# Placing the heads of four engines' loops at the first slot of an instruction block, in a Mamba kernel with a mixture of experts

## The chip, the cores and the metric

The kernel runs on one core of one Trainium2 chip. The metric is the device time of one execution in microseconds. Before the change its median over three runs is 8184.05 us (8180.95 to 8189.45). All arithmetic that matters here is in f32.

## The reference, cut to what matters

The input x is 4 sequences of 1024 tokens with 256 features. It is normalised, and then goes two ways: through eight Mamba layers, one after another, and through a mixture of eight experts of which each token takes one. The result is x plus the product of the first with the silu of the second.

```python
def _mamba_layer(x, Wi, cw, cb, Wx, Wdt, bdt, Alog, Dp, Wo):
    xz = einsum('bld,ed->ble', x, Wi); xin, z = split(xz, 2)
    xin = silu(causal_conv(xin, cw, cb))
    x_dbl = einsum('blc,ec->ble', xin, Wx)          # dt_raw, Bm, Cm
    delta = softplus(einsum('blr,cr->blc', dt_raw, Wdt) + bdt)
    y = selective_scan(delta, Bm, Cm, xin, -exp(Alog), Dp)   # h = h*exp(d*A) + d*u*B ; y = h.C
    return einsum('blc,dc->bld', y * silu(z), Wo)
for i in range(8):
    x = x + _mamba_layer(x, ...)
```

The scan has 512 channels and 16 states, and it is run over 1024 tokens of each of the 4 sequences in each of the 8 layers.

## The kernel before

The program has three stages. `experts` (up to about 520 us of the span) normalises and runs the mixture; `mamba` (to about 8116 us) runs the layers; `finish` multiplies and adds. The change is in `mamba`.

In `mamba` the work is cut into 64 units, numbered from 0: 8 layers by 4 sequences by 2 halves of 512 tokens. An even unit is a first half (h = 0) and an odd one a second half, which takes the scan's carry of the first. One unit is 16 states by 4 channel blocks, which makes 64 tiles of 128 partitions by 512 tokens. For each tile GpSimd makes the drive (L850), ScalarE the decay exp(delta A) into PSUM (L891), VectorE the scan (L1037). TensorE turns the state (L1192, four transposes an item) into one of two PSUM places, ScalarE weighs it with C (L898), and TensorE turns it back and adds it up in ps_y (L1199, four more). Between these, at places written out by hand (RING_AT, CONV_AT and the like), stand the projections of the next units, the convolution, the softplus and the gate. VectorE ends what it does ahead of a new unit with the second of two du products (L1085), and has the alive scan (L1059) some 20 us into the unit; the text uses these two as marks.

Each engine runs its own instruction stream, and semaphores order them. On TensorE, VectorE, ScalarE and GpSimd the units come from `units`: unit 0 and unit 1 are written out, then a loop of 30 iterations has two units in its body (units 2 to 61), and units 62 and 63 are written out again. L707 is the loop's line: its hint (the first instruction of the body), its counter and the compare-and-branch that closes it have that line in the trace. The branch is taken 29 times, always between an odd unit and the even one behind it. SyncE's stream, with all data transfers, is written out without a loop.

```python
        def units(eng, unit):
            unit(0, 0, 0, "first")
            unit(1, 1, 0, "mid")
            with nc.Fori(1, ITERS - 1, 1, engines=[eng.engine], hint_back_edge=True) as it:
                for h in range(HALVES):
                    unit(HALVES * it + h, h, it, "mid")
```

The instructions of an engine are 64 bytes each and are fetched from memory in blocks while it runs. In the compiled program the loop body, from its hint to its branch, has 2609 instructions on TensorE, 752 on ScalarE, 599 on VectorE and 344 on GpSimd. Counted from the start of each engine's own stream (the labels, which aren't loaded, left out) the bodies begin at instruction 6301 on TensorE, 1317 on ScalarE, 1122 on VectorE and 549 on GpSimd, and TensorE's branch is its instruction 8909. What the loader puts ahead of a stream comes on top of these and isn't in the program.

Of the kernel before, what the change touches and what calls it, by code (L numbers as in the profile page):

```python
# [40 lines left out]
ITERS = LAYERS * BATCH  # L41
# [596 lines left out]
def mamba(nc, w_in, w_x, w_dt, w_out, par, xres, ident, alive_dram, bc_dram):  # L638

    with ExitStack() as ctx:  # L640
# [62 lines left out]
        def units(eng, unit):  # L703

            unit(0, 0, 0, "first")
            unit(1, 1, 0, "mid")
            with nc.Fori(1, ITERS - 1, 1, engines=[eng.engine], hint_back_edge=True) as it:  # L707
                for h in range(HALVES):
                    unit(HALVES * it + h, h, it, "mid")
            unit(UNITS - 2, 0, ITERS - 1, "near")  # L710
            unit(UNITS - 1, 1, ITERS - 1, "last")
# [77 lines left out]
        def _(pool):  # L789
# [87 lines left out]
            halo(0, 0)  # L877
            mask_x(0, "pre1", 1, 1, 0)
            units(pool, unit)

        @block.scalar
        def _(act):
# [130 lines left out]
            exponent(0, 0, 0)  # L1013
            exponent(0, 0, 1)
            units(act, unit)
            for t in range(TC):
                weigh(UNITS, 0, "end", ("S", "prev", t), UNITS - 1, STATES - 1, t)

        @block.vector
        def _(dve):  # L1020
# [147 lines left out]
            for n in range(STATES):  # L1168
                for j in range(CB):
                    early(0, 1, "pre1", 1, 0, n, j)  # L1170
            units(dve, unit)
            for j in range(CB):
                gate(UNITS - 1, 1, j)
# [298 lines left out]
```

## Time and profile before

| | |
|---|---|
| median of 3 runs | 8184.05 us (8180.95 to 8189.45) |
| the profiled execution | 8167.01 us, span 8165.3 us |
| TensorE matmul, weight load | 6880.2 us (84%), 4850.8 us (59%) |
| VectorE | 6901.2 us (85%) |
| ScalarE | 6464.0 us (79%) |
| GpSimd | 6099.8 us (75%) |
| granted TensorE clock, mean | 0.959 |
| data transfers | 42 GB/s, 13.4% of the 16 engines' span |

The shares say how busy an engine is, not which one sets the time: no engine is full, and in each stretch of a unit another one comes last. The clock is a share of full speed, so that 0.5 is 1.2 GHz and 1.0 is 2.4 GHz. "issue" as a releaser means that the engine waited for nothing that the profile shows. Rows with a q behind the engine's name are of its sequencer.

### The profile page before, as it was taken

How to read it: one execution, taken by the hardware profiler on the slowest of the kernel's cores; microseconds unless marked ns; L12 is line 12 of the kernel's file. 1: busy time of each engine (PE TensorE's matmuls, PEld its weight loads, DVE VectorE, ACT ScalarE, POOL GpSimd, SP SyncE). 2: the span in 40 equal slices, each digit the busy share in tenths (PEclk: the TensorE clock that was granted, in tenths of full speed). 3: DMA queues.
4: the chain of work that ended last, by engine and by line, in shares of the span. 5: the costliest groups of instructions: out<-in, count | busy, mean ns of one | idle time of the engine just before them, and what ended most of it. 6: DMA issues, size and time to landing. Idle time of an engine off the chain costs nothing. (4 is left out here: it accounts for less than half of the span.)

```text
span 8165.3 us, 143446 instructions
## 1 busy us (share of the span) xinstructions
PE 6880.2 (84%) x39487; PEld 4850.8 (59%) x39551; DVE 6901.2 (85%) x6768; ACT 6464.0 (79%) x10250; POOL 6099.8 (75%) x5301
## 2 busy tenths in 40 slices
PE   6968888888888888888888888888888888888887
PEld 4645665565566556556655655665566566556555
DVE  3258988888898898889888888988888898888888
ACT  2258888888888888888888888888888888888887
POOL 2147787778788777778877777887778778778775
PEclk9979999999999999999999999999999999999998
DMA  4111111111111111111111111111111111111112
GB/s 155 33 34 37 37 37 42 39 36 38 39 42 40 35 38 42 39 36 38 38 41 39 36 38 39 41 40 36 36 42 40 36 38 39 40 39 37 37 37 88
DMA packets 201759, 345.60 MB, mean 42 GB/s; under 512 B 25152, under 2 KB 59744, under 8 KB 200832
## 3 DMA queue, kind: packets, MB, share of 16 engines
q1 hardware_dynamic: 197168, 325.46, 13.4%
q0 software_dynamic: 3792, 10.38, 0.4%
q8 instruction: 392, 6.42, 0.3%
q14 instruction: 407, 3.33, 0.1%
HBM read 318.04 MB, written 17.72 MB: 41 GB/s over the span
## 5 line engine op out<-in xcount | busy, mean ns | idle before, releaser
L850 POOL TENSOR_TENSOR drive<-du,brep 128x512 f32<-128x512 f32 x4096 | 5611.6, 1396 | 857.6 <-DVE du L1085 641.0
L891 ACT ACTIVATE ps_d<-delta,cur 128x512 f32<-128x512 f32 x4096 | 2827.5, 690 | 879.7 <-DVE state L1037 859.9
L898 ACT ACTIVATE prod<-ps_r,bcT 128x512 f32<-128x512 f32 x4096 | 2786.9, 680 | 353.6 <-PE ps_r L1192 343.0
L1192 PE MATMUL ps_r<-ident,state 128*128 128x128 f32 x16384 | 2613.4, 284 | 535.8 <-ACT prod L898 305.1
L1037 DVE TENSOR_TENSOR_SCAN state<-ps_d,carry,drive 128x512 f32<-128x512 f32 x2048 | 2519.5, 1265 | 281.7 <-ACT ps_d L891 143.5
L1037 DVE TENSOR_TENSOR_SCAN state<-ps_d,drive 128x512 f32<-128x512 f32 x2048 | 2398.4, 1205 | 395.1 <-ACT ps_d L891 203.3
L1199 PE MATMUL ps_y<-ident,prod 128*128 128x128 f32 x16384 | 2546.0, 281 | 106.5 <-issue 87.1
L1199 PEld LDWEIGHTS ps_y<-ident,prod 128*128 128x128 f32 x16384 | 1990.7, 145 | 773.2 <-issue 592.9
L1192 PEld LDWEIGHTS ps_r<-ident,state 128*128 128x128 f32 x16384 | 1906.0, 145 | 843.2 <-ACT prod L898 510.3
L1232 PE MATMUL ps_r<-xm,w_inx_sb 128*128 128x512 f32 x1024 | 529.9, 643 | 185.9 <-ACT prod L898 178.2
L1076 DVE SCALAR_TENSOR_TENSOR xc<-xpad,taps,xc 128x512 f32<-128x512 f32 x768 | 662.3, 862 | 2.9
L1240 PE MATMUL ps_r<-xm,w_inz_sb 128*128 128x512 f32 x1024 | 510.2, 621 | 126.1 <-ACT prod L898 125.8
L1269 PE MATMUL ps_r<-relu,w_out_sb 128*128 128x512 f32 x1024 | 468.4, 600 | 5.7 <-ACT prod L898 3.0
L1232 PEld LDWEIGHTS ps_r<-xm,w_inx_sb 128*128 128x128 f32 x1024 | 178.8, 194 | 377.3 <-issue 195.3
L836 POOL COPY carry<-state 128x4 f32<-128x4 f32 x512 | 175.1, 342 | 299.2 <-DVE state L1037 296.7
L1262 PE MATMUL ps_r<-xdbl,w_dt_sb 16*128 16x512 f32 x512 | 307.1, 682 | 80.6 <-ACT soft L944 51.4
L1240 PEld LDWEIGHTS ps_r<-xm,w_inz_sb 128*128 128x128 f32 x1024 | 174.6, 190 | 313.1 <-ACT prod L898 169.2
L1210 PE MATMUL ps_y<-u,skip 128*128 128x512 f32 x512 | 291.1, 711 | 20.7 <-DVE relu L1135 20.6
L1269 PEld LDWEIGHTS ps_r<-relu,w_out_sb 128*128 128x128 f32 x1024 | 184.2, 190 | 200.1 <-issue 187.0
L1248 PE MATMUL ps_r<-u,w_x_sb 128*48 128x512 f32 x512 | 236.4, 606 | 54.5 <-ACT u L916 54.5
L532 ACT ACTIVATE hid<-ps_t,b_sb 128x128 f32<-128x128 f32 x312 | 84.8, 382 | 227.5 <-PE ps_t L493 227.5
L460 POOL DMA_INDIRECT ys_dram<-yb,row x39 | 37.4, 958 | 296.7 <-DVE yb L552 296.7
(148 smaller groups left out, 4481.4 us busy)
## 6 DMA issues: line engine op xcount, KB each, us to landing
brep<-bc_dram SPq DMA_DIRECT2D x1024, 256.0 KB, 3.2
w_sb<-w SPq DMA_DIRECT2D x8, 1024.0 KB, 18.7
w_all<-w SPq DMA_DIRECT2D x8, 1024.0 KB, 13.7
xb<-xs_dram SPq DMA_DIRECT2D x39, 128.5 KB, 2.0
w_all<-x SPq DMA_DIRECT2D x4, 1024.0 KB, 9.3
w_inx_sb<-w_in SPq DMA_DIRECT2D x8, 512.0 KB, 4.0
w_inz_sb<-w_in SPq DMA_DIRECT2D x8, 512.0 KB, 4.0
w_out_sb<-w_out SPq DMA_DIRECT2D x8, 512.0 KB, 3.9
```

Source lines behind the costliest of these rows:

```text
L850: nc.gpsimd.tensor_tensor(drive[:, k % DRIVE, :], du[:, j, :], brep[:, n % BREP, :], ALU.mult).then_inc(drive_set, 1)
L891: nc.scalar.activation(ps_d[:, k % 2, :], delta[h][:, j, :], ACT.Exp, scale=cur[h][:, a:a + 1]).then_inc(decay_set, 1)
L898: nc.scalar.activation(prod[:, t, :], ps_r[:, item_place(U, h, kind, item), :], ACT.Copy, scale=bcT[(h + 1) % 2 if item[1] == "prev" else ...
L1037: nc.vector.tensor_tensor_scan(state[n % 2][:, j, :], ps_d[:, k % 2, :], drive[:, k % DRIVE, :], carry[:, n, j:j + 1] if h == 1 else 0.0, ...
L1076: step = nc.vector.scalar_tensor_tensor(xc[:, j, :], xpad[:, j, tap:tap + T], w, xc[:, j, :], ALU.mult, ALU.add)
L1192: last = nc.tensor.transpose(out[:, j * P:(j + 1) * P], state[n % 2][:, j, t * P:(t + 1) * P], ident[:])
L1199: last = nc.tensor.matmul(ps_y[:, j, t * P:(t + 1) * P], prod[:, t, j * P:(j + 1) * P], ident[:], start=False, stop=True, is_transpose=Tru ...
L1210: last = nc.tensor.matmul(ps_y[:, j, :], skip[:, j, :], u[:, j, :], start=True, stop=True, skip_group_check=True)
L1232: last = nc.tensor.matmul(out, w_inx_sb[:, k, j * P:(j + 1) * P], xm[h][:, k, :], start=(k == 0), stop=(k == DB - 1))
L1240: last = nc.tensor.matmul(out, w_inz_sb[:, k, j * P:(j + 1) * P], xm[hf][:, k, :], start=(k == 0), stop=(k == DB - 1))
L1262: nc.tensor.matmul(out, w_dt_sb[:, j * P:(j + 1) * P], xdbl[0:RANK, :], start=True, stop=True).then_inc(ring_ready, 1)
L1269: last = nc.tensor.matmul(out, w_out_sb[:, j, k * P:(k + 1) * P], gated[:, j, :], start=(j == 0), stop=(j == CB - 1))
```

## The change

The loop gets one more argument, which asks the loader to put the body's first instruction, on each of the four engines, at slot 0 of a block of 256 instruction slots (and so of a block of 128 as well). The slots skipped ahead of it are padding, and the stream jumps over them once. No instruction in the body is added, removed or moved against another, and no wait or buffer changes.

```diff
-            with nc.Fori(1, ITERS - 1, 1, engines=[eng.engine], hint_back_edge=True) as it:
+            with nc.Fori(1, ITERS - 1, 1, engines=[eng.engine], hint_back_edge=True,
+                         head_slot={eng.engine: 0}) as it:
                 for h in range(HALVES):
                     unit(HALVES * it + h, h, it, "mid")
```

## Rows read from the trace of the kernel before

**Rows 1.** The page, DMA queues of kind instruction: packets, MB, share of 16 engines.
```profile
q8 instruction: 392, 6.42, 0.3%
q14 instruction: 407, 3.33, 0.1%
```
**Rows 2.** Line L707 by engine: count, ns min/median/max, first and last start in us.
```profile
L707 PEldq COMPARE_BRANCH  x30: 87/3588/3933, 998.0 to 7899.1; - x30
...
L707 ACTq COMPARE_BRANCH  x30: 44/49/68, 998.6 to 7899.8; - x30
...
L707 DVEq COMPARE_BRANCH  x30: 61/68/90, 995.6 to 7896.7; - x30
...
L707 POOLq COMPARE_BRANCH  x30: 44/49/70, 983.5 to 7884.7; - x30
```
**Rows 3.** The waits: who waited for what, us in total, times, longest.
```profile
PE ps_y L1199 <- issue: 87.1, 26, 3.7
```
**Rows 4.** Timeline of PE around the turn into unit 14: start, length, instructions, idle before.
```profile
2181.25 0.62 PE L1192 MATMUL ps_r<-ident,state 128*128 128x128 f32 x4
...
2187.39 0.66 PE L1192 MATMUL ps_r<-ident,state 128*128 128x128 f32 x4 [1.12 <-ACT zs L910]
2191.59 1.11 PE L1199 MATMUL ps_y<-ident,prod 128*128 128x128 f32 x4 [3.54 <-issue]
```
**Rows 5.** The DMA view of 2187.4 to 2188.6 us, the instruction queue.
```profile
q8 instruction: 1, 0.02, 7.6%
```
**Rows 6.** Line L707 on TensorE's sequencer, 2184 to 2192 us.
```profile
L707 PEldq COMPARE_BRANCH  x1: 3823/3823/3823, 2187.5 to 2187.5; - x1
```
**Rows 7.** The DMA view of 2899 to 2900 us, ahead of the turn into unit 20.
```profile
q8 instruction: 1, 0.02, 7.5%
```
**Rows 8.** Line L707 on TensorE's sequencer, 2898 to 2903 us.
```profile
L707 PEldq COMPARE_BRANCH  x1: 1397/1397/1397, 2900.8 to 2900.8; - x1
```
**Rows 9.** Timeline of PE behind the turn into unit 20.
```profile
2905.66 0.33 PE L1192 MATMUL ps_r<-ident,state 128*128 128x128 f32 x1 [1.30 <-issue]
```
**Rows 10.** Windows: stretch, length, busy PE PEld DVE ACT POOL, clock, DMA share, GB/s.
```profile
2191.00:2194.00 3.00, 2.41 (x12) 2.41 (x13) 1.41 (x2) 0.31 (x1) 3.00 (x4) 0.50 0.30 79
...
2902.00:2905.00 3.00, 1.85 (x15) 1.62 (x15) 3.00 (x4) 1.88 (x4) 3.00 (x3) 1.00 0.03 8
```
**Rows 11.** Timeline of DVE: du and alive marks, turns into units 2, 14, 15, 20, 23.
```profile
757.82 1.20 DVE L1085 TENSOR_TENSOR du<-delta,u 128x1024 f32<-128x1024 f32 x1
778.57 1.19 DVE L1059 TENSOR_TENSOR_SCAN alive<-ps_r,zeros 128x512 f32<-128x512 f32 x1
...
2187.20 1.19 DVE L1085 TENSOR_TENSOR du<-delta,u 128x1024 f32<-128x1024 f32 x1
2211.98 1.19 DVE L1059 TENSOR_TENSOR_SCAN alive<-ps_r,zeros 128x512 f32<-128x512 f32 x1
...
2308.40 1.20 DVE L1085 TENSOR_TENSOR du<-delta,u 128x1024 f32<-128x1024 f32 x1
2330.36 1.25 DVE L1059 TENSOR_TENSOR_SCAN alive<-ps_r,alive,zeros 128x512 f32<-128x512 f32 x1
...
2900.54 1.19 DVE L1085 TENSOR_TENSOR du<-delta,u 128x1024 f32<-128x1024 f32 x1
2923.70 1.19 DVE L1059 TENSOR_TENSOR_SCAN alive<-ps_r,zeros 128x512 f32<-128x512 f32 x1
...
3257.51 1.20 DVE L1085 TENSOR_TENSOR du<-delta,u 128x1024 f32<-128x1024 f32 x1
3284.58 1.28 DVE L1059 TENSOR_TENSOR_SCAN alive<-ps_r,alive,zeros 128x512 f32<-128x512 f32 x1 [0.97 <-PE ps_r L1223]
```
**Rows 12.** Timeline of DVE: more du marks, into units 3, 12 and 13.
```profile
875.06 1.20 DVE L1085 TENSOR_TENSOR du<-delta,u 128x1024 f32<-128x1024 f32 x1
...
1950.73 1.19 DVE L1085 TENSOR_TENSOR du<-delta,u 128x1024 f32<-128x1024 f32 x1
...
2070.79 1.20 DVE L1085 TENSOR_TENSOR du<-delta,u 128x1024 f32<-128x1024 f32 x1
```

## The prediction

> **What bounds the kernel now.** I read the page first. It has no full engine, so the shares don't decide, and its chain of waits covers only the last 50 us. The change touches nothing but where code lies, so I then looked for rows of instruction fetch and of the loop's own line. The page has two queues of kind instruction. One moves 6.42 MB in 392 packets, which is 16.4 KB each, or 256 instructions of 64 bytes; the other 3.33 MB in 407, or 128 instructions each [rows 1]. I take the first queue to be TensorE's, since only TensorE executes enough instructions to fill it (16384 of one kind alone), and the second to be the other engines'.
>
> The view of line L707 shows what closing the loop costs. On ScalarE, VectorE and GpSimd the branch takes 49, 68 and 49 ns. On TensorE its median is 3588 ns and its longest 3933; only the last, which isn't taken, is 87 ns [rows 2]. The waits show the same from the other side: 26 idle times of TensorE with no releaser, 87.1 us in all [rows 3]. Of the 29 taken branches 26 are like the one at 2187.5 us and 3 are like the one at 2900.8.
>
> In the long case TensorE has 3.54 us with nothing to do [rows 4], while the branch stands for 3.82 us [rows 6] and one 16 KB packet of its queue is moved [rows 5]. The packet starts behind the branch's start. In the short case the packet starts between 2899 and 2900 us [rows 7], ahead of the branch at 2900.8, and the branch takes 1.40 us [rows 8]. A fetch that only a missed branch can start can't begin ahead of the branch. So I read it this way: the hint works, the block of the target is fetched once the sequencer is in the branch's own block, but TensorE enters that block only a few instructions ahead of the branch. The counts allow it. TensorE's branch is instruction 8909, and 35 blocks are 8960, so if the loader puts about 51 to 60 instructions ahead of the stream the branch lies in one of the first slots of its block. This offset is inferred, not shown.
>
> **What a turn costs.** The stall reaches the time if VectorE is late by it. I take the two marks on VectorE on either side of the turn [rows 11]:
> - long branch (unit 14): 2187.20 to 2211.98, 24.78 us; 25 of the 26 long ones lie within 0.05 us of it, one has 25.12.
> - short branch (unit 20): 2900.54 to 2923.70, 23.16 us; the other two are within 0.02.
> - no branch (unit 2, the same code, entered from straight code): 757.82 to 778.57, 20.75 us.
>
> So a long turn costs 24.78 - 20.75 = 4.03 us, more than the branch itself, and a short one 23.16 - 20.75 = 2.41 us. Two further rows say why it is more. Behind a long branch TensorE's clock is at 0.50, that is at 1.2 GHz, after the idle stretch; behind a short one it is at 1.00, 2.4 GHz [rows 10]. And behind the short one TensorE stops again for 1.30 us with no releaser [rows 9], some 36 instructions into the body, where by the same offset it crosses into the next block, whose fetch could only start once the head's block was there.
>
> **The change part by part.** *TensorE.* With the head at slot 0 the body of 2609 ends 2608 slots on; 10 blocks are 2560, so the branch is at slot 48 of its block. Counting 48 instructions back from the branch through weight loads and matmuls leads into the group at 2181.25 us [rows 4], 6.2 us ahead of the branch at 2187.5 [rows 6]. The fetch needs what the long branch takes, 3.9 us at most with the packet. It is hidden with 2.3 us to spare; without that cover up to 3.9 us a turn would remain. The branch should take about 0.09 us, its untaken price [rows 2]. The first crossing behind the head moves from some 40 to 256 instructions on, so the stop of 1.30 us goes too. What is late next at the turn is what is late in unit 2. Sum: 26 x 4.03 + 3 x 2.41 = 112.0 us gained. The bound from below is the mark distance of a turn between halves with no branch, unit 15, 2308.40 to 2330.36 = 21.96 us [rows 11]: 26 x 2.82 + 3 x 1.20 = 76.9 us. I take unit 2, since unit 15 has scans with a carry and other code.
>
> *The rest of an even unit.* From mark to mark unit 2 takes 875.06 - 757.82 = 117.24 us [rows 11, 12], so 96.49 behind its alive scan. Unit 14 takes 2308.40 - 2187.20 = 121.20, so 96.42. Unit 12 takes 2070.79 - 1950.73 = 120.06, and with the same first part 95.28 [rows 11, 12]. Which of the two an even unit gets depends on where low-clock stretches fall, and the change moves them. Of the 26 even units behind long branches the mean of this part is 95.6. If all became like unit 2, 29 x 0.9 = 26 us of the gain would be lost; if all became like unit 12, 29 x 0.3 = 9 us would come on top. I take no change and keep both ends: 86 to 121 us.
>
> *ScalarE, VectorE, GpSimd.* They lose nothing now [rows 2], so nothing can be gained at their branches. With heads at slot 0 their branches lie 111, 86 and 87 slots into blocks of 128 (752, 599 and 344 less one, less whole blocks). An iteration of some 238 us over 752 slots gives ScalarE 0.3 us a slot, so its last block is entered some 35 us ahead. The work of those slots hides a fetch of 3.9 us; if it didn't, it would be up to 3.9 us a turn. I set it at 0.
>
> *Entering the loop.* One jump over padding on each engine, once. If its target block isn't there it is one fetch, 0 to 3.9 us. I take 2 us, as ScalarE feeds every scan.
>
> *Data transfers.* SyncE has no loop and isn't touched; its waits come sooner with the rest.
>
> Net: 112 - 2 = 110 us. The profiled execution would go from 8167.0 to 8057 us. The median of the runs is 17 us above it, an offset that I keep: 8184.05 - 110 = 8074 us.
>
> **A page's rule against the change.** The same rows 2 show three engines whose loops are longer than what one or two blocks hold (ScalarE's 752 are 5.9 blocks of 128) and which still branch back in 49 to 68 ns. The Trainium skill, Runtime: NRT & Kernel Launch, section Instruction fetch mechanics, says that a taken branch to a target outside the current two-page window forces a fetch before execution can go on. By that rule TensorE's branch would stall wherever the head lies, and the time would stay at 8184 us; the trace disagrees with it on three engines out of four.
>
> **The rivals.**
> - *The turn still waits* (the head isn't moved, or TensorE's fetch starts at the branch in any layout). For it: 26 packets start behind the branch. Against it: the 3 that start ahead of it, and three engines that don't wait. Time 8184 us. Chance 0.07.
> - *The turn becomes like the one between halves*: another engine takes over at 21.96 us. Net 76.9 - 2 = 75, time 8109 us. For it: no branch stands between halves either, and those turns are at 21.96 us. Against it: unit 2, the same code as all even units, at 20.75. Chance 0.08.
> - *Slower: low-clock stretches early in the units.* Unit 23 has no branch and still takes 3284.58 - 3257.51 = 27.07 us between marks, with a wait for TensorE at its end, 5.1 us more than unit 15 [rows 11]. If shorter iterations lock to a phase in which one unit of every iteration has this, it costs 30 x 5.1 = 153 us against 110 gained: 8227 us. It decides from 22 of 30 iterations on. Only units 3 and 23 of 64 have it now. Chance 0.03.
> - *The forecast*, 8074 us, with its own range of 8063 to 8100 by the ends above. Chance 0.82.
>
> **How the numbers follow.** The range takes the forecast's ends, some us for the offset between profile and runs, and the second rival: 8055 to 8115 us. It leaves out the first and third, 0.10. A measurement of this kernel can tell about 0.2%, 16 us, from no change. Faster by more: 0.82 + 0.08 = 0.90. Within: 0.07. Slower: 0.03.
>
> **What would show it.** TensorE's branches near 0.09 us; the row of 26 idle times without a releaser gone; even units at about 20.75 us between the marks; the clock at 1.00 behind the turn. Branches still above 1 us would refute the reading of the offset; branches at 0.09 us with the marks at 22 us or more would mean that another engine took over; a gain at the turns that is lost again behind the alive scan would be the clock. I am wrong outright if another engine's branch grows to microseconds.

## The result, and the profile after

| | before | after |
|---|---|---|
| median | 8180.95 us (5 runs, 8177.64 to 8189.45) | 8153.57 us (5 runs, 8142.65 to 8172.95) |
| the profiled execution | 8167.01 us, span 8165.3 | 8159.41 us, span 8157.4 |
| mean clock | 0.959 | 0.959 |

The ratio is 0.9966, with an interval of 0.995 to 0.9983. The kernel is faster by 27 us, not by the 110 that I predicted, and the time lies above the range of 8055 to 8115. Behind L707 the lines are one higher than before: the scan is now L1038, the alive scan L1060, du L1086, the transposes L1193 and L1200.

The page's queues of kind instruction and the loop's line, as in [rows 1, 2]:

```profile
q8 instruction: 363, 5.95, 0.3%
q14 instruction: 381, 3.12, 0.1%
...
L707 POOLq COMPARE_BRANCH  x31: 33/49/70, 740.0 to 7878.1; - x31
L707 DVEq COMPARE_BRANCH  x31: 57/68/92, 752.3 to 7890.1; - x31
L707 PEldq COMPARE_BRANCH  x31: 88/3359/3895, 754.8 to 7892.5; - x31
L707 ACTq COMPARE_BRANCH  x31: 38/49/73, 755.5 to 7893.1; - x31
```

The head did move. Each engine has one branch record more, the jump over the padding, and TensorE fetches 29 packets fewer, 11 instead of 12 per trip, because a body of 2609 instructions that starts at slot 0 touches 11 blocks. But TensorE's branch still has a median of 3359 ns. The row of the waits that was to vanish is nearly what it was in [rows 3]:

```profile
PE ps_y L1200 <- issue: 86.1, 28, 3.7
```

The turn into unit 14, the counterpart of [rows 4 to 6]: timeline of PE, TensorE's branch, the instruction queue in the DMA view of 2182.8 to 2184 us, and the two marks on DVE.

```profile
2181.84 0.66 PE L1193 MATMUL ps_r<-ident,state 128*128 128x128 f32 x4 [1.12 <-ACT zs L911]
2185.57 1.11 PE L1200 MATMUL ps_y<-ident,prod 128*128 128x128 f32 x4 [3.07 <-issue]
...
L707 PEldq COMPARE_BRANCH  x1: 3351/3351/3351, 2181.9 to 2181.9; - x1
...
q8 instruction: 1, 0.02, 5.2%
...
2181.65 1.19 DVE L1086 TENSOR_TENSOR du<-delta,u 128x1024 f32<-128x1024 f32 x1
2206.44 1.19 DVE L1060 TENSOR_TENSOR_SCAN alive<-ps_r,zeros 128x512 f32<-128x512 f32 x1
```

The DMA view of 2175 to 2182.8 has no packet of q8. So the packet of the target starts behind the branch's start, as before. The turn is 24.79 us long, as before (24.78).

The turn into unit 18 is one of three with a short branch, the counterpart of [rows 7 to 9]. Its packet is in the DMA view of 2656.5 to 2658.2 us, ahead of the branch.

```profile
q8 instruction: 1, 0.02, 4.0%
...
L707 PEldq COMPARE_BRANCH  x1: 1140/1140/1140, 2658.3 to 2658.3; - x1
...
2658.20 0.66 PE L1193 MATMUL ps_r<-ident,state 128*128 128x128 f32 x4 [1.12 <-ACT zs L911]
2659.71 0.65 PE L1200 MATMUL ps_y<-ident,prod 128*128 128x128 f32 x4 [0.86 <-issue]
2660.20 0.60 PE L1193 MATMUL ps_r<-ident,state 128*128 128x128 f32 x4
...
2658.00 1.19 DVE L1086 TENSOR_TENSOR du<-delta,u 128x1024 f32<-128x1024 f32 x1
2678.78 1.19 DVE L1060 TENSOR_TENSOR_SCAN alive<-ps_r,zeros 128x512 f32<-128x512 f32 x1
```

This turn is 20.78 us, where the short ones before were 23.16 [rows 11]. The second stop of 1.30 us [rows 9] is gone: the first crossing into a new block now lies 256 instructions into the body. The windows behind the two turns (columns as in [rows 10]) show the clock at 1.2 GHz behind the long branch and at 2.4 GHz behind the short one:

```profile
2186.00:2189.00 3.00, 3.00 (x16) 3.00 (x15) 0.89 (x2) 1.27 (x2) 3.00 (x3) 0.50 0.42 92
2660.00:2663.00 3.00, 2.73 (x26) 2.50 (x25) 3.00 (x3) 1.98 (x4) 3.00 (x3) 1.00 0.03 5
```

Where the time of the two profiled executions went, from the marks of the 29 even units behind a branch: the turns' mean fell from 24.62 to 24.35 us (7.8 us in all), the rest of the even units rose from 95.57 to 95.97 (11.6 lost), the odd units fell by 0.17 each (4.8), and all that lies outside gives some 6. That makes 7 of the 7.6 us between the two executions. The medians are 27 us apart. The profiled execution of before, 8167.0 us, is shorter than each of its five runs (8177.6 to 8189.5), which that of after isn't; how many of the branches are short in executions without a profile isn't known, and so the other 20 us have no rows.

### The profile page after: what moved, and what is told of

Read it like the earlier page. It is cut to its first block and busy times, and to the rows that moved or that the text cites. A ratio compares the mean times of both kernels' runs of the same rounds, so it can differ in the third digit from the quotient of the medians.

```text
span 8157.4 us, 143514 instructions
## 1 busy us (share of the span) xinstructions
PE 6897.5 (85%) x39551; PEld 4858.0 (60%) x39551; DVE 6894.2 (85%) x6768; ACT 6470.4 (79%) x10250; POOL 6107.9 (75%) x5301
## 5 line engine op out<-in xcount | busy, mean ns | idle before, releaser
L1193 PE MATMUL ps_r<-ident,state 128*128 128x128 f32 x16384 | 2611.0, 284 | 523.2 <-ACT prod L899 302.4
L1038 DVE TENSOR_TENSOR_SCAN state<-ps_d,carry,drive 128x512 f32<-128x512 f32 x2048 | 2521.3, 1266 | 279.0 <-ACT ps_d L892 144.7
L1038 DVE TENSOR_TENSOR_SCAN state<-ps_d,drive 128x512 f32<-128x512 f32 x2048 | 2399.9, 1206 | 397.2 <-ACT ps_d L892 215.6
L1200 PE MATMUL ps_y<-ident,prod 128*128 128x128 f32 x16384 | 2554.2, 282 | 105.2 <-issue 86.1
L1200 PEld LDWEIGHTS ps_y<-ident,prod 128*128 128x128 f32 x16384 | 1995.8, 145 | 779.6 <-issue 597.6
L1193 PEld LDWEIGHTS ps_r<-ident,state 128*128 128x128 f32 x16384 | 1909.6, 145 | 828.1 <-ACT prod L899 507.5
```

Source lines behind the costliest of these rows:

```text
L1038: nc.vector.tensor_tensor_scan(state[n % 2][:, j, :], ps_d[:, k % 2, :], drive[:, k % DRIVE, :], carry[:, n, j:j + 1] if h == 1 else 0.0, ...
L1193: last = nc.tensor.transpose(out[:, j * P:(j + 1) * P], state[n % 2][:, j, t * P:(t + 1) * P], ident[:])
L1200: last = nc.tensor.matmul(ps_y[:, j, t * P:(t + 1) * P], prod[:, t, j * P:(j + 1) * P], ident[:], start=False, stop=True, is_transpose=Tru ...
```

## The experiments

All edits are made to the kernel after. E1 to E4 share their runs of before (median 8163.15 us), E5 to E8 theirs (8164.28), E9 to E11 theirs (8157.26); E12 has its own (8160.68). The four groups ran on four chips, and the change's own before is 8180.95, so that ratios are compared across them and not microseconds. Branches, packets and turns are read from one profiled execution of each kernel. A crossing is the place where TensorE's stream passes from one block of 256 slots into the next, and a block is entered when the first instruction behind the crossing is executed. The question is why a fetch whose block was entered 6.2 us ahead of the branch still comes late, and from where on it doesn't.

**E1: TensorE's head at slot 128, its branch at slot 176.**

```diff
-                         head_slot={eng.engine: 0}) as it:
+                         head_slot={eng.engine: 128 if eng.engine == mybir.EngineType.PE else 0}) as it:
```

> TensorE's loop head is at slot 128 of its block of 256 instead of slot 0, so that its closing branch (2608 instructions on) is at slot 176 instead of 48. The other three heads stay at slot 0. Theory A (the fetch for the hinted target starts only some 40 to 110 instructions after the branch's block is entered, as the fetches behind the other block crossings of the changed kernel do): all 29 branches near 0.09 us, turns into even units at 20.8 us between the marks, 26 x 4.0 us less than the changed kernel, so about 8153.6 - 104 = 8050 us. Theory B (on TensorE the fetch of a hinted target waits for the branch itself, and the three early ones are chance): 26 branches still at 3.3 to 3.9 us, time 8154 us.

Measured: 8035.87 us (8034.94 to 8040.89), ratio 0.9845 (0.9829 to 0.9861). Line L707, the instruction queue in the DMA view of 2143.5 to 2145 us, the branch of the same turn, and its marks:

```profile
L707 PEldq COMPARE_BRANCH  x31: 88/357/382, 758.6 to 7765.9; - x31
...
q8 instruction: 1, 0.02, 3.9%
...
L707 PEldq COMPARE_BRANCH  x1: 357/357/357, 2159.4 to 2159.4; - x1
...
2159.11 1.20 DVE L1086 TENSOR_TENSOR du<-delta,u 128x1024 f32<-128x1024 f32 x1
2179.85 1.19 DVE L1060 TENSOR_TENSOR_SCAN alive<-ps_r,zeros 128x512 f32<-128x512 f32 x1
```

The packet of the target starts 15 us ahead of the branch in all 29 turns, the row of idle time without a releaser is gone, and every turn is as long as the one of unit 2 before, 20.74 to 20.86 us. The Trainium skill, Runtime: NRT & Kernel Launch, section Instruction fetch mechanics, would make a taken branch with its target outside a two-page window wait for a fetch. Here 29 branches go back over ten blocks in at most 0.38 us, so the measurement decides against that rule for a loop with a hint.

**E2: TensorE's head at slot 64, branch at slot 112.**

```diff
+                         head_slot={eng.engine: 64 if eng.engine == mybir.EngineType.PE else 0}) as it:
```

> TensorE's loop head at slot 64, the closing branch at slot 112. Theory A: the fetch starts ahead of the branch in most or all turns, but may not have ended; branches between 0.09 and some 1.5 us, turns at 20.8 us, time 8050 to 8080 us. Theory B: 8154 us, branches at 3.3 to 3.9 us.

Measured: 8050.09 us (8044.98 to 8064.71), ratio 0.9859 (0.9842 to 0.9875).

```profile
L707 PEldq COMPARE_BRANCH  x31: 88/367/1708, 756.9 to 7792.0; - x31
```

The 29 branches fall into two groups. In 15 the packet starts 12 us ahead, and they take 0.36 to 0.38 us; in 14 it starts 1.3 us ahead, and they take 1.04 to 1.71 us. The block of the branch was entered 10 us ahead in both. So the lag from the entry to the start of the fetch differs from turn to turn: -2 us in 15 of them, 8.6 to 9.1 in 14. The profiled execution took 8064.71 us and is the longest of the four, so the median of 8050 may stand for turns that divide otherwise.

The short stops also show what a stop costs. Turns into units 16 and 20: windows behind the branch, the branches, and the marks of unit 20.

```profile
2399.00:2402.00 3.00, 3.00 (x21) 3.00 (x19) 3.00 (x4) 2.54 (x5) 3.00 (x4) 0.66 0.16 29
2868.70:2871.70 3.00, 2.56 (x22) 2.08 (x21) 3.00 (x3) 2.99 (x5) 3.00 (x3) 1.00 0.16 48
...
L707 PEldq COMPARE_BRANCH  x1: 1039/1039/1039, 2396.4 to 2396.4; - x1
L707 PEldq COMPARE_BRANCH  x1: 1064/1064/1064, 2866.0 to 2866.0; - x1
...
2865.68 1.19 DVE L1086 TENSOR_TENSOR du<-delta,u 128x1024 f32<-128x1024 f32 x1
2886.46 1.19 DVE L1060 TENSOR_TENSOR_SCAN alive<-ps_r,zeros 128x512 f32<-128x512 f32 x1
```

Two stops of the same length, 1.04 and 1.06 us. With the clock at 2.4 GHz behind it the turn is 20.78 us, as without a stop; where a stretch at 1.2 GHz follows, it is 23.18. All 14 divide so: nine at full clock have 20.76 to 20.79 us, five with the low clock 23.17 to 24.82. A stop of up to 1.55 us at full clock is covered.

**E3: head at slot 192, branch at slot 240.** The edit is that of E1 with 192.

> TensorE's loop head at slot 192, the closing branch at slot 240; the first crossing behind the head comes after 64 instructions. Theory A: branches near 0.09 us as with slot 128; the first crossing is short of room, so a stop of TensorE of up to 1.3 us some 60 instructions behind the turn may come back, without the half clock: turns at 20.8 to 21.5 us, time 8050 to 8070 us. Theory B: 8154 us.

Measured: 8037.78 us (8034.97 to 8041.59), ratio 0.9845 (0.9828 to 0.9861); branches `88/357/382`, turns 20.78 us. The packet starts 14.0 to 20.7 us ahead of the branch in all 29 turns. The first crossing, now 64 instructions into the body, costs nothing either: the stop that was expected as possible didn't come, and the time is below the expected 8050 to 8070.

**E4: only TensorE's head is placed, at slot 0.**

```diff
+                         head_slot={eng.engine: 0} if eng.engine == mybir.EngineType.PE else None) as it:
```

> Only TensorE's head is at slot 0; ScalarE's, VectorE's and GpSimd's lie where they fall, as in the kernel before. Both theories: the three other branches cost 0.05 to 0.07 us before and after, so their heads are worth nothing, and the time is that of the changed kernel, 8154 us, within 10 us. If the gain of 27 us came from the other engines' heads, it is 8181 us.

Measured: 8139.57 us (6 runs, 8131.59 to 8147.29), ratio 0.9971 (0.9958 to 0.9983), the same as the change's 0.9966 within the intervals; 25 long branches and 4 short. In microseconds it is 14 below the expected 8154, on a chip where before is 18 lower too. The other three heads bring nothing that can be measured.

**E5 and E6: the two sides of the block's edge.** Heads at slots 207 and 208 put the branch at slot 255 and at slot 0 of the next block. The edit is that of E1 with 207 and with 208.

> TensorE's head at slot 207, its branch at slot 255, the last of its block: the block is entered 255 instructions ahead of the branch. Theory A (lateness of the block's entry decides): branches at 0.36 us as with slots 128 and 192, turns at 20.8 us, ratio to the kernel before 0.985. Rival C (it is the first crossing behind the head, 49 instructions on, that decides, or the place near the block's end): as the kernel before, ratio 1.0, branches at 3.3 us or more.

> TensorE's head at slot 208, one slot further, its branch at slot 0 of the next block: the block is entered with the branch itself. Theory A: the fetch can't have started, 26 or more of 29 branches at 3.3 us or more, turns at 24.8 us, ratio to the kernel before 1.00, some 125 us slower than slot 207. Rival C: like slot 207.

Measured: E5 8039.06 us (8036.4 to 8046.41), ratio 0.9846 (0.9829 to 0.9862). E6 8162.21 us (10 runs, 8143.43 to 8163.55), ratio 0.999 (0.9981 to 1.0). L707 of E5 above, of E6 below, with E6's waits and its instruction queue:

```profile
L707 PEldq COMPARE_BRANCH  x31: 88/357/382, 758.5 to 7777.4; - x31
```

```profile
L707 PEldq COMPARE_BRANCH  x31: 87/3555/3834, 758.5 to 7898.1; - x31
...
PE ps_y L1200 <- issue: 95.3, 29, 3.6
...
q8 instruction: 393, 6.44, 0.3%
```

One slot is worth 123 us. Blocks of 256 slots are real, they are counted as the change counts them, and a branch at the first slot of a block is late 29 times of 29. This fits the kernel before, whose branch was in one of the first slots of its block by the stop of [rows 9].

**E7: slot 128, and no hints on any engine.**

```diff
-            with nc.Fori(1, ITERS - 1, 1, engines=[eng.engine], hint_back_edge=True,
-                         head_slot={eng.engine: 0}) as it:
+            with nc.Fori(1, ITERS - 1, 1, engines=[eng.engine], hint_back_edge=False,
+                         head_slot={eng.engine: 128 if eng.engine == mybir.EngineType.PE else 0}) as it:
```

> Heads as in the run with slot 128, but without the hints at the loop's top (one instruction less in each body). Theory A: a hint with a late fetch is worth no more than no hint. TensorE's 29 branches at 3.3 to 3.9 us, turns at 24.8 us or more, and ScalarE's and VectorE's branches at 3 us or more too, GpSimd's at 0.05 us (its body is not refetched). Ratio 1.00 to the kernel before where the stalls overlap, up to 1.01 where VectorE's own comes on top. If the hint is without effect on TensorE: 0.985.

Measured: 8162.24 us (10 runs, 8156.16 to 8178.7), ratio 1.0 (0.999 to 1.0009). L707 and the two queues:

```profile
L707 PEldq COMPARE_BRANCH  x31: 83/3697/4070, 759.2 to 7905.9; - x31
L707 ACTq COMPARE_BRANCH  x31: 38/45/54, 759.9 to 7906.6; - x31
...
q8 instruction: 393, 6.44, 0.3%
q14 instruction: 437, 3.58, 0.1%
```

Without the hint all of E1's gain is gone, and TensorE moves one packet more per trip than E1 (393 against 365): this fits a fetch that runs on into the block behind the loop and goes to the target only once the branch is executed. The hint turns it in time. ScalarE's branch record stays at 45 ns although its target isn't there: its next record of L707 comes 2.7 us behind the branch in the median, VectorE's 2.9, against 0.41 and 0.52 with the hint. In this view a short branch doesn't prove that nothing waited, and my reading of [rows 2] for the three other engines rested on it. The edit takes the hint from all four engines, so the time alone doesn't say which of them costs; TensorE's records and turns of 24.8 us, as before, do.

**E8: TensorE's head at 128, VectorE's at slot 46**, which puts VectorE's branch at slot 4 of a block of 128.

```diff
+                         head_slot={eng.engine: {mybir.EngineType.PE: 128, mybir.EngineType.DVE: 46}.get(eng.engine, 0)}) as it:
```

> TensorE's head at slot 128 as in the fastest run so far, and VectorE's at slot 46, so that VectorE's branch lies at slot 4 of a block of 128 (46 + 598 = 5 x 128 + 4). Theory A, if it holds for VectorE: its 29 branches go from 0.07 to some 3 us, and the time rises by 29 x 2 to 29 x 3.5 us, to about 8036 + 60 to 100 = 8096 to 8136 us. If its fetch isn't late or another wait hides it: 8036 us.

Measured: 8033.03 us (8031.62 to 8054.5), ratio 0.9847 (0.983 to 0.9865). L707 on VectorE in one turn of E8, and in the same turn of E1:

```profile
L707 DVEq COMPARE_BRANCH  x1: 68/68/68, 2159.4 to 2159.4; - x1
L707 DVEq BRANCH_PREFETCH_HINT  x1: 39/39/39, 2161.7 to 2161.7; - x1
```

```profile
L707 DVEq COMPARE_BRANCH  x1: 68/68/68, 2157.1 to 2157.1; - x1
L707 DVEq BRANCH_PREFETCH_HINT  x1: 39/39/39, 2157.6 to 2157.6; - x1
```

From branch to hint it is 2.30 us in the median (2.23 to 2.48), against 0.52. VectorE's sequencer is late by some 1.8 us a turn, and the mean turn stays at 20.77 us. VectorE has a scan and a product queued when it branches, about 2.4 us, behind the one that runs. The delay also bears on the block's size: in blocks of 256 this branch would be at slot 132, about 50 us behind the crossing at 238 us for 599 slots (an estimate), and no delay would be expected.

**E9 and E12: slots between.** Heads at 32 and 96, branches at slots 80 and 144. The edit is that of E1 with 32 and with 96.

> Head of TensorE's loop at slot 32 of a block of 256 (branch at slot 80), the other heads at 0. The loop branch has been seen at slots 48, 112 and 176: 3, 15 and 29 of 29 target packets started ahead of it. Theory 'the place of the branch in its block sets how much time the fetch has, and its start lags the entry of the block by a time that varies from turn to turn': slot 80 lies between 48 and 112, so 4 to 14 of 29 branches under 2 us, turn mean between 24.35 and 21.53, time between 8050 and 8150, most likely near 8110. Theory 'every branch that is not a whole further block away misses alike, and the 15 of slot 112 are chance': 3 or 4 early, 8150.

> Head of TensorE's loop at slot 96 of a block of 256 (branch at slot 144), the other heads at 0. So far the branch at slots 48, 80, 112 and 176 gave 3, 12, 29 and 29 of 29 branches under 2 us, and 0, 4, 15 and 29 of 29 under 0.5 us; the fetch started up to some 10 us behind the entry of the block. Theory 'the branch must lie far enough behind the crossing to cover that lag, and more distance always helps': at slot 144 at least 25 of 29 under 0.5 us, no branch above 1.7 us, turns of 20.78 to 21.2, 8034 to 8046 us, ratio 0.985. Rival 'what counts is where in the body the crossing falls, not the distance': any number of branches under 0.5 us, also fewer than 15, and a time anywhere from 8036 to 8100.

Measured: E9 8104.64 us (8100.71 to 8132.94), ratio 0.9945 (0.9927 to 0.9963). E12 8040.74 us (8037.9 to 8055.41), ratio 0.9858 (0.9842 to 0.9875). L707 of E9, then of E12:

```profile
L707 PEldq COMPARE_BRANCH  x31: 88/3099/3612, 757.3 to 7835.9; - x31
```

```profile
L707 PEldq COMPARE_BRANCH  x31: 88/438/461, 756.3 to 7773.1; - x31
```

These fill the curve. "Entered" is how long ahead of the branch TensorE executed the first instruction of the branch's block (good to some 0.4 us, since matmuls and the sequencer's records lie a few places apart); the fetch's start is that of the target's packet against the branch's start; both come from the records of TensorE's instructions and of its instruction queue, 29 turns each.

| run | slot | entered | fetch starts (turns) | under 0.5 / to 2 / over 2 us | mean turn | median |
|---|---|---|---|---|---|---|
| E6 | 0 | 0 | +0.9 to +1.4 (29) | 0 / 0 / 29 | 24.76 | 8162 |
| after | 48 | -6.1 | +0.7 to +1.5 (26), -1.3 (3) | 0 / 3 / 26 | 24.35 | 8154 |
| E9 | 80 | -8.0 | +0.7 to +1.3 (17), -1.3 (8), -5.6 to -7.0 (4) | 4 / 8 / 17 | 23.04 | 8105 |
| E2 | 112 | -10.0 | -0.9 to -1.4 (14), -12 (15) | 15 / 14 / 0 | 21.53 | 8050 |
| E12 | 144 | -13.7 | -5.7 to -7.0 (28), -12.6 (1) | 29 / 0 / 0 | 20.96 | 8041 |
| E1 | 176 | -15.2 | -15.3 to -15.8 (29) | 29 / 0 / 0 | 20.78 | 8036 |
| E3 | 240 | -20.0 | -14.0 to -20.7 (29) | 29 / 0 / 0 | 20.78 | 8038 |
| E5 | 255 | -21.7 | -15.7 to -23.8 (29) | 29 / 0 / 0 | 20.79 | 8039 |

Slot 80 gave 12 branches under 2 us, inside the 4 to 14 of the first theory, and slot 144 gave 29 of 29. The more slots lie between the crossing and the branch, the fewer turns are late, and from 144 on none is. The rival of E12, that only the place in the body counts, isn't needed for the branches, but it isn't dead for the lag: that is -2 to 9 us from E2's crossing, 4.8 to 7.6 from the change's, and about zero from E1's.

**E10: only TensorE's head is placed, at slot 128.**

```diff
+                         head_slot={eng.engine: 128} if eng.engine == mybir.EngineType.PE else None) as it:
```

> Only TensorE's head is placed, at slot 128 (branch at slot 176); ScalarE, VectorE and GpSimd stay where the kernel before has them. Theory 'only TensorE's branch is waited for': as with all four placed, 8036 (8033 to 8042), ratio 0.985, branches of 0.36 us, turns of 20.78. Rival 'with TensorE's stop gone the other engines' branches are next in line, and their heads at slot 0 helped': 8045 to 8060.

Measured: 8043.21 us (8035.24 to 8046.52), ratio 0.986 (0.9844 to 0.9877). That is one us above the upper end of the expected 8033 to 8042, with an interval that overlaps E1's; the profiled execution has a span of 8033.5 us against E1's 8034.1, branches `88/357/382` and turns of 20.77. One head on one engine is the whole effect.

**E11: TensorE's head at 128, ScalarE's at slot 21**, which puts ScalarE's branch at slot 4 of a block of 128.

```diff
+                         head_slot={eng.engine: {mybir.EngineType.PE: 128, mybir.EngineType.Activation: 21}.get(eng.engine, 0)}) as it:
```

> TensorE's head at 128; ScalarE's head moved so that its branch stands at slot 4 of a block of 128, only four instructions behind the crossing. Both theories expect ScalarE's next own record to come late behind its branch, some 2.3 us instead of 0.41, as it did on VectorE with its branch at slot 4. Theory 'work already queued on the engine covers it': VectorE had 2.4 us queued and lost nothing; ScalarE has one or two activations of about 0.7 us queued, so 1 to 1.7 us per turn come to light and 29 turns cost 0 to 45 us, most likely 30: 8066. Rival 'ScalarE has slack in the turn whatever is queued': 8036 as with the head at 0.

Measured: 8043.04 us (8037.96 to 8050.77), ratio 0.9857 (0.984 to 0.9873), against E10's 8043.21 on the same chip: no cost in the medians. The profiled execution, 8050.77 us, has two turns of 25.8 us, with the clock at 1.2 GHz late in the turn and branches of 0.36 us. L707 on ScalarE in one turn of E11, and in the same turn of E1:

```profile
L707 ACTq COMPARE_BRANCH  x1: 49/49/49, 2161.9 to 2161.9; - x1
L707 ACTq BRANCH_PREFETCH_HINT  x1: 31/31/31, 2162.7 to 2162.7; - x1
```

```profile
L707 ACTq COMPARE_BRANCH  x1: 49/49/49, 2160.1 to 2160.1; - x1
L707 ACTq BRANCH_PREFETCH_HINT  x1: 31/31/31, 2160.5 to 2160.5; - x1
```

Both theories had expected a delay of some 2.3 us, and it is 0.3 to 0.6. So the run doesn't tell them apart: the cover was hardly asked for. It shows only that four slots behind a crossing were nearly enough on ScalarE, which takes about 0.3 us per slot, where on TensorE 48 slots weren't.

## Why the prediction was wrong

**Right: the branch is the cost, and the hint can remove it.** E1 takes the branches to 0.36 us and E7 puts them back.

**Right: the price of a turn and its bound.** I took 4.03 us for a long turn, from unit 2's 20.75. In E1 the mean turn is 20.78 against 24.62 before, 29 x 3.84 = 111.4 us, where my sum had 112.0. E1's medians are even 127 us apart, and the spans of the two profiled executions 131. These say where the rest is: the odd units are shorter by 0.52 us each in the mean (15 us) and the first units by 5. The rival in which another engine takes over at 21.96 us fell with this.

**Right: the stop behind the short branch.** With the head at slot 0 it is gone, and the three short turns are at 20.78 us.

**Right: the other engines' heads.** E4 and E10 show them worth nothing. The reason that I gave, "they lose nothing now", leaned on the branch's own record, which E7 shows to be blind on ScalarE and VectorE. It holds all the same: in the kernel before, the next own record comes 0.41 and 0.52 us behind the branch, against 2.7 and 2.9 where the fetch is late.

**Wrong: "The fetch needs what the long branch takes, 3.9 us at most with the packet. It is hidden with 2.3 us to spare."** This one step carries nearly the whole error. The fetch itself is shorter than I said: from the packet's start to the end of the branch it is 2.3 to 2.8 us in the kernels before and after. But I let it start with the entry of the block. In the kernel after the block is entered 6.1 us ahead and the packet starts 6.8 to 7.6 us behind that in 26 of 29 turns, some 1 us behind the branch's start. I had no row for the time between entry and start, and took it as nothing without saying so. The trace of before did have it. With the block's edge where the stop of [rows 9] puts it, some 36 to 40 instructions into the body, each trip has eleven crossings, and by the records the packets start between 3.8 us ahead of the crossing instruction and 8.8 behind it; at one crossing the median is 8.2 us. Set against the 6.2 us of cover, these would have said that slot 48 is too early.

**The sum redone.** Three short turns at 20.78 instead of three at 23.15, and 26 long ones as before: 7 us, which is what the turns of the profiled executions give (7.8).

**The rival that came closest** was "the turn still waits", at 0.07, but its reason ("TensorE's fetch starts at the branch in any layout") is refuted by E1. It should have been split: starts at the branch always, or starts too late for 48 slots.

**Wrong, small: the branch at 0.09 us.** The untaken branch is no price for a taken one; with the target there it takes 0.36 us. It costs nothing here.

**Small, and too low: entering the loop at 2 us.** The jump over the padding does meet a target that isn't there. ScalarE jumps at 755.5 us, and the first instruction of its body comes at 758.2:

```profile
L707 ACTq BRANCH_PREFETCH_HINT  x30: 31/31/55, 758.2 to 7658.9; - x30
```

The turn into unit 2 is 24.92 us in the kernel after, where it was 20.75: 4.2 us in place of 2, once. In the other kernels with four placed heads it is 23.15 to 24.94, and in E4 and E10, where only TensorE jumps, 20.77 and 20.78. Little of it need reach the time: from the mark into unit 2 to that into unit 4, E1 and E10 both take 234.8 us.

**Still open:** what sets the lag on TensorE. It isn't one number: it depends on the crossing, and for one crossing it can take two values (E2). The records hold a trace of a cause that no run tested. Where the packet of the target starts ahead of the branch, it often starts while TensorE waits for another engine: in the kernel after 3 of 3 times, in E2, E5 and E10 29 of 29, in E1 24. In E2 the two values are two such waits, both for ScalarE, of 1.0 us some 12 us ahead of the branch and of 1.1 us directly ahead of it. Such waits fill some 27% of the 16 us ahead of a branch. But in E12 it is 6 of 29 and in E3 7, so this is no rule. The unexplained 20 us between the medians of before and after are open as well.

## What to carry to other kernels

- For a hinted loop on an engine that waits at its branch, choose the slot of the branch, not that of the head: here the slots tried from 144 on (144, 176, 240 and 255 of 256), with 13.7 us or more between the crossing and the branch, hid the fetch in every turn of the profiled executions. A head at slot 0 leaves the branch wherever the body's length puts it.
- When a fetch or any other prefetch is called hidden, look in the trace for the time between what allows it and its first packet, at all places where it happens. Its own duration isn't the cover that it needs.
- A sequencer can wait behind its branch record. Read the distance to the loop's next own record, and ask what was queued on the engine.

## What the runs showed that I had not expected

- **The turn's length doesn't follow the stop's.** In the kernel after, branches from 3.08 to 3.90 us all give turns of 24.8 us, but for one each of 23.58 and 25.18. Stops of 1.06 to 1.55 us at full clock (E2) give 20.78, as none does. What goes with the longer turns is the stretch at 1.2 GHz behind the stop: it was there behind all 26 long branches of the kernel after and all 17 of E9, and in five of 14 short ones of E2. It isn't the only cause: two of E2's 15 early branches have full clock behind them and turns of 24.81 us, with a low stretch near the turn's end. The 13 kernels with placed heads agree: a turn with no stretch at 1.2 GHz between its marks is 20.73 to 20.79 us long, with stops of up to 1.63 us as with none, and every turn above 20.86 has such a stretch, among them two of about 25.8 us in E11 and one in E12, which have branches of 0.36 and 0.44 us. The two short turns of before with full clock throughout, 23.15 and 23.16, are the exception, and they have the second stop of [rows 9]. Every stop above 3 us comes with the low clock, so how much of the 4.0 us is the clock and how much the stop was not separated.
- **One slot, 123 us** (E5 and E6): a branch at the last slot of its block has the most time, a branch at the first slot of the next has none.
- **An engine can branch late without anyone noticing** (E8): some 1.8 us late in each turn, at no cost, which fits the 2.4 us of work that it had queued.
